# A graph network's second round: one of four parts of the dst one-hots is made by GpSimd instead of VectorE

## The reference

```python
h = jnp.maximum(_layernorm(x, axis=-1), 0.0)
for t in range(num_rounds):                 # 2 rounds
    src = x[row]
    dest = x[col]
    m_input = jnp.concatenate([dest, src, edge_attr], axis=1)
    messages = m_input @ msg_W[t].T + msg_b[t]
    agg = jax.ops.segment_sum(messages, row, num_segments=x.shape[0])
    x = _gru_cell(agg, x, gru_Wih[t], gru_bih[t], gru_Whh[t], gru_bhh[t])
```

## Time and profile before

| | us |
|---|---|
| median of three runs | 2292.99 |
| lowest and highest run | 2291.53, 2293.34 |
| the profiled execution | 2290.76 |
| its span from first to last instruction | 2288.8 |
| VectorE busy, whole span | 2132.3 (93%) |
| ScalarE busy | 1894.5 (83%) |
| TensorE matmul busy | 1507.7 (66%) |
| GpSimd busy | 743.5 (32%) |

### The profile page before, as it was taken

How to read it: one execution, slowest core, us unless ns; L and a number is a source line. 1 busy time by engine, 2 the same in 40 slices (tenths; PEclk the granted TensorE clock), 3 DMA queues, 4 the chain that set the end, 5 groups by cost and what they waited for, 6 DMA issues and landing times. The chain is left out here.

```text
span 2288.8 us, 121076 instructions
## 1 busy us (share of the span) xinstructions
PE 1507.7 (66%) x43734; PEld 1405.6 (61%) x43734; DVE 2132.3 (93%) x3394; ACT 1894.5 (83%) x4474; POOL 743.5 (32%) x1245
## 2 busy tenths in 40 slices
PE   0000000000024899999999999958999999999996
PEld 0000000000013899999999999858999999999996
DVE  8999999999967899999999999958999999999996
ACT  4778795664124899999999999958999999999996
POOL 1000000000085666666666666621222222122222
PEclk9999999999999999999999999979999999999998
DMA  6100001210233676666667777636767777777773
GB/s 124 34 0 0 0 0 36 47 23 22 56 91 88 210 228 231 221 233 228 228 233 226 229 229 229 217 124 215 244 240 240 240 240 240 239 241 239 240 241 118
DMA packets 165648, 375.64 MB, mean 164 GB/s; under 512 B 70877, under 2 KB 87427, under 8 KB 165023
## 3 DMA queue, kind: packets, MB, share of 16 engines
q1 hardware_dynamic: 114427, 191.07, 26.9%
q0 software_dynamic: 49456, 181.94, 24.0%
q10 hardware_dynamic: 1708, 1.97, 0.3%
HBM read 358.39 MB, written 16.17 MB: 164 GB/s over the span
## 5 line engine op out<-in xcount | busy, mean ns | idle before, releaser
L1399 ACT ACTIVATE rows<-ps_rows 128x512 f16<-128x512 f32 (+1 forms) x2744 | 1362.3, 612 | 53.3 <-PE ps_rows L1298 42.9
L1503 DVE TENSOR_TENSOR src<-iota_units,src_lane 128x2048 f16<-128x2048 f16 (+2 forms) x784 | 801.4, 1022 | 26.6 <-PE ps_sum L1318 19.2
L1320 PE MATMUL ps_sum<-rows,src 128*64 128x132 f16 x10192 | 555.9, 222 | 9.0 <-issue 1.6
L1298 PE MATMUL ps_rows<-rows_next,planes 128*64 128x128 f16 x10192 | 535.4, 219 | 36.4 <-DVE planes L1499 21.3
L1298 PE MATMUL ps_rows<-rows_now,planes 128*64 128x128 f16 x10192 | 545.8, 219 | 19.7 <-ACT rows L1399 9.2
L1318 PE MATMUL ps_sum<-src,rows 128*64 128x128 f16 x10192 | 542.0, 220 | 4.8 <-ACT rows L1399 1.2
L1499 DVE TENSOR_SCALAR planes<-planes,lane_no 128x2048 f16<-128x2048 f16 (+2 forms) x784 | 515.8, 658 | 8.7 <-DMA planes<-lanes_dram 8.6
L816 PE MATMUL ps_src<-ident,late 104*64 104x104 f32 x98 | 19.9, 380 | 642.0 <-DVE late L1051 623.4
L1298 PEld LDWEIGHTS ps_rows<-rows_now,planes 128*64 128x64 f16 x10192 | 412.2, 110 | 41.1 <-ACT rows L1399 17.9
L1298 PEld LDWEIGHTS ps_rows<-rows_next,planes 128*64 128x64 f16 x10192 | 397.8, 109 | 60.6 <-DVE planes L1499 21.9
L816 PEld LDWEIGHTS ps_src<-ident,late 104*64 104x64 f32 x98 | 13.7, 162 | 648.1 <-DVE late L1051 624.0
(11 more groups left out here) (213 smaller groups left out, 2200.3 us busy)
## 6 DMA issues: line engine op xcount, KB each, us to landing
planes<-lanes_dram POOLq DMA_DIRECT2D x196, 512.0 KB, 4.4
planes<-lanes_dram SPq DMA_DIRECT2D x194, 512.0 KB, 4.6
planes<-lanes_dram POOLq DMA_DIRECT2D x98, 448.0 KB, 4.6
planes<-lanes_dram SPq DMA_DIRECT2D x97, 448.0 KB, 4.6
planes<-lanes_dram POOLq DMA_DIRECT2D x98, 192.0 KB, 3.7
planes<-lanes_dram SPq DMA_DIRECT2D x97, 192.0 KB, 3.9
rows_now<-parts_dram SPq DMA_DIRECT2D x104, 32.0 KB, 1.7
rows_next<-parts_dram SPq DMA_DIRECT2D x104, 32.0 KB, 3.5
```

The lines of the kernel that those rows point to most:

```text
L1298: last = nc.tensor.matmul(ps_rows[(u + NU * b) % 4][half * SLOTS:(half + 1) * SLOTS, k * 2 * H:(k + 1) * 2 * H], dst1[q][:, (c - 2 * QUART ...
L1320: last = nc.tensor.matmul(ps_sum[b][at, 0:width], hot[:, at], row, start=(j == 0), stop=(j == J - 1))
L1399: nc.scalar.activation(rows_of_unit(u, b)[:, :, 0:2 * H], cut(ps_rows[(u + NU * b) % 4][:])[:, 0:n, :], ACT.Copy).then_inc(rows_ready, 1)
L1503: nc.vector.tensor_tensor(src1[q][:], iota_units[:].rearrange("p (o l) k -> p o l k", o=1) .broadcast_to([P, pairs_now, P, 2]), src_lane[: ...
```

## The change

In the second round GpSimd makes `dst1[3]`, the part of 768 columns, in its own body ahead of the copy of h. It counts it on a semaphore of its own. VectorE makes the other three parts of `dst1` and all four of `src1`. TensorE and SP, who wait for `dst1`, wait for either semaphore, depending on the part. To make room for the new semaphore, VectorE's three chains of steps now count on one.

```diff
 class Chain:
-    def __init__(self, engine, sem):
-        self.engine, self.sem, self.at = engine, sem, 0
+    def __init__(self, engine, sem, at=0):
+        self.engine, self.sem, self.at = engine, sem, at
...
-                step = Chain(dve, dve_edges)
+                step = Chain(dve, dve_own, setup_chain[0].at)
...
-                step = Chain(dve, dve_spread)
...
+            dst1_last_ready = path_sem(f"dst1_last_ready{r}") if flipped else None
+            dst1_parts = NQ - 1 if flipped else NQ
+
+            def await_dst1(engine, s, q):
+
+                if q < dst1_parts:
+                    wait(engine, dst1_ready, s * dst1_parts + q + 1)
+                else:
+                    wait(engine, dst1_last_ready, s + 1)
 
             def fetch_lanes(engine, s):
                 for q in range(NQ):
-                    engine.wait_ge(dst1_ready, (s - 1) * NQ + q + 1)
+                    await_dst1(engine, s - 1, q)
                     fetch_some_lanes(engine, s, r, q)
...
+                    def last_one_hot(s):
+
+                        q = NQ - 1
+                        pool.wait_ge(lanes_in[q], 16 * s + 16)
+                        wait(pool, gathered, done_with(s, q))
+                        plain(nc.gpsimd.tensor_scalar(dst1[q], lanes[q], lane_no[:, 0:1], None,
+                                                      ALU.is_equal)).then_inc(dst1_last_ready, 1)
+
                     if not more:
                         def body(s, b, half):
+                            last_one_hot(s)
                             copy_now(s, b)
...
                     def gather(s, u, b):
                         q = u // UQ
                         if u % UQ == 0:
-                            te.wait_ge(dst1_ready, s * NQ + q + 1)
+                            await_dst1(te, s, q)
...
                     def one_hots(s, q):
-                        dve.wait_ge(lanes_in[q], 16 * s + 16)
-                        wait(dve, gathered, done_with(s, q))
-                        nc.vector.tensor_scalar(dst1[q], lanes[q], lane_no[:, 0:1], None,
-                                                ALU.is_equal).then_inc(dst1_ready, 1)
+                        if q < dst1_parts:
+                            dve.wait_ge(lanes_in[q], 16 * s + 16)
+                            wait(dve, gathered, done_with(s, q))
+                            nc.vector.tensor_scalar(dst1[q], lanes[q], lane_no[:, 0:1], None,
+                                                    ALU.is_equal).then_inc(dst1_ready, 1)
```

More of the change, by code:

```diff
@@ L327, in build @@
         EARLY = 2 * (NB // 14)
+        setup_chain = []
         prep_scope = ctx.enter_context(ExitStack())
@@ L444, in _ @@
                 step = Chain(dve, dve_own)
+                setup_chain.append(step)
                 nc.vector.memset(w_node[:], 0.0).then_inc(cleared, 1)
@@ L536, in build @@
         windows_in = sem("windows_in")
-        dve_edges = sem("dve_edges")
         pads_ready = sem("pads_ready")
@@ L713, in build @@
         lanes_out = sem("lanes_out")
-        dve_spread = sem("dve_spread")
         check_ready = sem("check_ready")
```

## The result

The changed kernel takes 2307.24 us (median of 4 runs, 2306.68 to 2308.22) against 2292.26 for the kernel before (four runs as well; the 2292.99 given above is the median of the first three): ratio 1.0068, 95% interval 1.0054 to 1.0081. The forecast was 2315 us, slower; the range held the time.

What follows compares the result with a forecast made beforehand. TensorE and ScalarE set the pace; VectorE would become the bound: -0.33 + 0.72 - 0.12 = 0.27 us a tile over 90 tiles, less its lead, adds 21.5 us, giving 2315 us, slower. Range 2293 to 2375 us.

Steps and rivals of the forecast that it cites:

- The bound: Second round: TensorE and ScalarE set the pace together; VectorE runs ahead and becomes the bound 0.12 us a tile above present work.
- What the move takes from VectorE: Second round: one 768-column instruction a tile leaves VectorE, 0.33 us from start to start, by itself worth nothing in time.
- The turn: VectorE is held up beside GpSimd's new 768-column comparison, charged at 0.72 us a tile.
- the select's slope: GpSimd's one-input select, 0.94 ns a column, used to price the 768-column comparison at 0.72 us.
- my upper price: GpSimd's two-input add, 1.95 ns a column, giving 1.50 us for 768 columns and a time of 2385 us.
- The spare time: Second round: VectorE's waits for TensorE, 9.2 us in 550 us, leave it 0.12 us a tile.
- The count: 90 of the second round's 98 tiles pay 0.27 us each, 24.3 us; VectorE's lead of 2.8 us comes off: 21.5 us.
- GpSimd's own queue: GpSimd's comparison waits behind earlier copy, add and store, ready just at TensorE's limit; later lane fetches only use up VectorE's lead.
- The slow comparison: Rival: GpSimd's comparison costs 1.45 ns a column, a turn of 1.11 us, 56 us more, 2349 us; chance 27%.
- VectorE paying too little: Rival: VectorE pays less than 0.45 us a tile, so TensorE and ScalarE keep the pace, 2293 us; chance 15%.
- GpSimd late for TensorE: Rival: TensorE waits for the last part in every second tile, some 0.3 us a pair, 13 us, 2306 us; chance 10%.
- The signs: Second round: VectorE's wait for TensorE gone, tile about 7.65 us, ScalarE some 95% busy, VectorE neighbours stretched about 0.7 us.

Runs made afterwards that it cites:

- e2: Changed kernel, but GpSimd compares only 2 of the 768 columns of the last part, all waits and hand-overs kept: 2291.89 us, ratio 1.0009 to the kernel before.
- e3: Kernel with all one-hots back on VectorE, plus one extra 768-column VectorE comparison a tile into a scratch tile in the second round: 2289.64 us, ratio 1.0006.
- e5: Changed kernel, but GpSimd makes the last part in even tiles only, VectorE in odd tiles: 2290.13 us, ratio 1.0002 to the kernel before.
- e10: As e5, and in odd tiles VectorE instead of ScalarE copies the turned tile out of PSUM: 2284.82 us, ratio 0.9976 to the kernel before.
- e11: As e5, and in every tile VectorE instead of ScalarE copies the turned tile out of PSUM: 2288.65 us, ratio 0.9991 to the kernel before.
- e6: Changed kernel, but GpSimd makes the last part in odd tiles only, VectorE in even tiles: 2293.14 us, ratio 1.0016 to the kernel before.

## Why the prediction came out as it did

**The bound.** Right. VectorE was off the path with little spare time, relief of it is worth nothing (e2), and it became the bound: of the 15.018 us of a pair none is VectorE's waiting.

**What the move takes from VectorE**, 0.33 us a tile: right; the extra comparison in e3 shows the same distance.

**The turn**, 0.72 us a tile: measured 0.65. A mean pair after is 15.018 us, VectorE's own work in it 14.14 - 0.66 = 13.48, so 1.54 us are turns; some 0.25 of them belong to the add (0.84 for 0.66 at 1910.02) and the copies (0.07); 1.29 us are left for two comparisons. The size was nearly right and the way to it was not. I had taken the select's slope for the whole length of the comparison. The comparison takes 2.22 us alone, (2.22 - 0.44) / 704 = 2.5 ns a column, above even my upper price, and VectorE is charged only for turns of 0.6 us, none, one or two. Two mistakes offset each other.

**The spare time**, 0.12 us a tile: too small. GpSimd's add and copies had taken 0.38 us a pair and take 0.25 now, which adds 0.06 a tile. Summed again: -0.33 + 0.65 - 0.12 - 0.06 = 0.14 us a tile against 0.27 forecast; measured (15.018 - 14.756) / 2 = 0.13. So the turn was taken 0.07 us a tile too dear and the room 0.06 too small, about equally. But the room fails more widely: in e3 it was off by 0.2 us a tile.

**The count.** 90 tiles by 0.13 are 12 us, and the lead of 2.8 us that I took off did not show. The profiled spans differ by 16.5 us. The same GRU step, pair by pair, stands 1.2 us later than before at the end of the first round (there the other runs, whose first round is the same code, stand between -1.8 and 1.6, so this is not the move), 3.1 us at 1610 us, 14.5 us at 2230 us and 14.0 us at the last pair. The last 2.5 us are in the tail: GpSimd's queue is behind, and the last add waits for the store ahead of it, where before it waited for VectorE's last step (first row before, second after):

```profile
2274.88 0.42 POOL L1239 TENSOR_TENSOR out_rows<-attr_room,h 128x128 f32<-128x128 f32 x1 [1.53 <-DVE h L1555]
...
2290.46 0.42 POOL L1247 TENSOR_TENSOR out_rows<-attr_room,h 128x128 f32<-128x128 f32 x1 [1.45 <-DMA out_dram<-out_rows]
```

I had not priced that end. So the 16.5 us are 1.2 of the first round, 1.9 up to 1610 us, 11.5 in the 42 pairs up to 2230 us, 0.6 given back after that, and 2.5 in the tail. The sum had forecast 21.5 us for the steady part alone, nearly twice what it gave; that the total came nearer is luck.

**GpSimd's own queue.** The order that I gave was wrong. It came of a slip in the description of the kernel: the copy of tile T waits for T - 1 turns, the last of which is that of tile T - 2, and TensorE makes that one at unit 1 of its tile T. So by the next tile the copy is done and the comparison stands first: 1906.48, then copy 1909.39 and add 1909.65. What it waits for is its lanes. Only 72.1 us in the waits are put down to them and 153.7 us to TensorE. But in the trace the lanes land at 1906.21 and 1913.58, 0.27 us before these two comparisons, and 0.26 to 0.28 us lie between landing and start in the five others from 1876 to 1923 us. The conclusion held: in that tile it is ready at 1909.42, and TensorE takes it at 1911.47.

**The rivals.** The slow comparison is true of its length and false of its price to VectorE. The Trainium skill's page "GPSIMD Engine Reference", section "3.1 Elementwise — side-by-side cycle accounting", has 769 ns for 512 elements, about 1.5 ns each; this comparison took 2.5 ns a column. The other page, "SBUF — State Buffer", section "Who interferes with whom", pointed to the right place, and its distinction of reads from writes for two-input instructions, which the prediction left out, fits the memset's 0 against 0.56 us. Its sentence that the pair is held for the whole instruction does not fit the comparison; the measurement decides. VectorE paying too little is true only for even tiles alone (e5). GpSimd late for TensorE: no steady wait of that kind.

**The signs.** VectorE's wait for TensorE is gone and its neighbours are stretched, as I had said. The tile takes 7.51 us and not 7.65, ScalarE is busy 98% and not 95%, and the stretch is not 0.7 us each time but 1.25 or 0.14.

## What to carry to other kernels

Before work is moved to GpSimd, look at what VectorE runs at the time it will fall: where it met VectorE's PSUM reads it cost 0.14 us, beside instructions with SBUF operands alone 0.6 or 1.2 us, for an instruction worth 0.33 us to VectorE. Even in the better place it gained nothing (e5, e10, e11). Relief of an engine off the path is worth nothing; here ScalarE was on it, and a copy moved from ScalarE to VectorE in every second tile gave 8 us. The idle time in the list of waits is a lower bound of an engine's room where some of its instructions are stretched by a neighbour: compare stretched and plain distances from start to start first.

## What the runs showed that I had not expected

The cost of a meeting is not a constant: it was 0.14, some 0.5 or 1.25 us, and in e6 two comparisons that began within 0.05 us of the same place cost 1.24 and 0.58 us. A comparison of f16 on GpSimd takes 2.22 us for 768 columns where a copy takes 0.82 and a memset 0.74 us. A memset beside VectorE's tensor_tensor form costs it nothing.
